# Pairwise tower: a clear of 192 in place of 64 scratch columns between gathers, a fourth group looked up by one-hot columns, groups transposed singly

## The reference, cut to what matters

```python
e = stack([tbl_f[ids[:, f]] for f in range(32)], axis=1)      # 1024 x 32 x 64
p, q = e[:, ROW], e[:, COL]                                   # 496 pairs, r < c
kp = einsum('bpj,ipj->bpi', p, kernel)                        # a 64x64 matrix per pair
z = sum(kp * q, axis=-1)                                      # 1024 x 496
h = concatenate([z, dense_ctx], axis=1)                       # 1024 x 512
h = maximum(h @ W_top1 + b_top1, 0); h = maximum(h @ W_top2 + b_top2, 0)
y = h @ W_top3
```

## Time and profile before

| | |
|---|---|
| median of 3 executions | 626.92 us (626.18 to 627.76) |
| profiled execution, its own time | 622.16 us |
| span of its trace | 620.2 us |
| PE, DVE, POOL, ACT busy | 502.4, 305.6, 273.9, 67.4 us |
| mean granted TensorE clock | 0.884 |
| gathers | 244, 950 to 1089 ns each |

### The profile page before, as it was taken

How to read it: one execution, slowest core, us unless ns; L and a number is a source line. 1 busy time by engine, 2 the same in 40 slices (tenths; PEclk the granted TensorE clock), 3 DMA queues, 4 the chain that set the end, 5 groups by cost and what they waited for, 6 DMA issues and landing times.

```text
span 620.2 us, 10322 instructions
## 1 busy us (share of the span) xinstructions
PE 502.4 (81%) x4290; PEld 309.4 (50%) x4290; DVE 305.6 (49%) x324; ACT 67.4 (11%) x130; POOL 273.9 (44%) x492
## 2 busy tenths in 40 slices
PE   1764444589999786678898768699889999999998
PEld 0432200356666454446565435466566666766443
DVE  3611200166776364337455436467377788787000
ACT  0001000011111021011001001011001211100112
POOL 5888887555557676352727445555700000000000
PEclk9975655599999998798978879899989999999999
DMA  5521212033331111010101011010100030000000
GB/s 154 179 71 23 58 23 61 18 90 90 104 109 43 31 24 26 13 25 9 22 16 23 15 23 28 17 22 17 22 12 1 14 110 10 2 10 2 0 0 0
DMA packets 15318, 23.56 MB, mean 38 GB/s; under 512 B 5506, under 2 KB 7810, under 8 KB 15145
## 3 DMA queue, kind: packets, MB, share of 16 engines
q1 hardware_dynamic: 6884, 14.14, 7.8%
q0 software_dynamic: 7808, 8.01, 6.5%
q10 hardware_dynamic: 580, 0.76, 0.4%
HBM read 20.79 MB, written 0.00 MB: 34 GB/s over the span
## 4 chain that ended last, share of the span: by engine, by line
PE 67%; another core or an unknown queue 13%; issue 10%; DVE 7%; DMA 2%; ACT 0%; SPq 0%; DVEq 0%
PE kp L539 37%; PE z_ps L556 19%; DVE prod L485 6%; PE kp L577 4%; PE tr_ps L523 3%; PE kp L583 2%; PE tr_ps L515 2%; DMA k_sb<-in_tbl 2%; DVE prod L495 1%; PE kp L590 0%; ACT pair L397 0%; ACT prod L441 0%; DVEq L484 0%; SPq L334 0%
## 5 line engine op out<-in xcount | busy, mean ns | idle before, releaser
L485 DVE TENSOR_TENSOR prod<-kp,pair 128x1024 f32<-128x1024 f32 x224 | 261.4, 1218 | 239.0 <-PE kp L539 137.7
L539 PE MATMUL kp<-pair,k_sb 64*128 64x256 f32 x1984 | 286.7, 420 | 63.8 <-issue 32.4
L377 POOL DMA_INDIRECT raw<-in_tbl,ids_sb x244 | 232.8, 954 | 174.8 <-PE tr_ps L523 99.9
L539 PEld LDWEIGHTS kp<-pair,k_sb 64*128 64x128 f32 x1984 | 202.8, 203 | 138.8 <-issue 69.5
L556 PE MATMUL z_ps<-prod,ones_sel 128*32 128x256 f32 x1984 | 141.5, 389 | 24.2 <-issue 22.5
L556 PEld LDWEIGHTS z_ps<-prod,ones_sel 128*32 128x32 f32 x1984 | 65.0, 111 | 94.5 <-issue 57.3
L397 ACT ACTIVATE pair<-tr_ps 128x512 f32<-128x512 f32 (+1 forms) x40 | 20.5, 512 | 351.5 <-PE tr_ps L523 249.4
L381 POOL MEMSET rest<- 128x64 f32 x244 | 40.9, 168 | 0.4
L495 DVE TENSOR_TENSOR prod<-kp,pair 128x512 f32<-128x512 f32 x48 | 30.2, 683 | 8.9 <-issue 6.6
L523 PE MATMUL tr_ps<-ident,raw 128*128 128x128 f32 x122 | 23.8, 309 | 11.4 <-issue 10.8
L515 PE MATMUL tr_ps<-prod,k_sb 125*64 125x256 f32 x96 | 16.6, 521 | 15.7 <-DMA k_sb<-in_tbl 13.4
(11 more groups left out here) (10 smaller groups left out, 9.0 us busy)
## 6 DMA issues: line engine op xcount, KB each, us to landing
k_sb<-in_kd SPq DMA_DIRECT2D x15, 512.0 KB, 3.7
raw<-in_tbl,ids_sb POOLq DMA_INDIRECT x244
pair<-pair SPq DMA_DIRECT2D x32, 64.0 KB
k_sb<-in_tbl SPq DMA_DIRECT2D x6, 250.0 KB
k_sb<-in_w SPq DMA_DIRECT2D x1, 1024.0 KB, 5.0
hot_ids_sb<-in_hot_ids SPq DMA_DIRECT2D x3, 250.0 KB
z_sb<-in_dense ACTq DMA_DIRECT2D x1, 512.0 KB
k_sb<-in_w SPq DMA_DIRECT2D x1, 512.0 KB, 5.7
```

What stands on the lines that cost most here:

```text
L377: nc.gpsimd.indirect_dma_start(raw[:, r % RAW_RING, i, n, :], None, tables[f], bass.IndirectOffsetOnAxis(ap=ids_sb[:, 2 * b + i, f:f + 1], ...
L485: nc.vector.tensor_tensor(prod[:, u % PROD_RING, :, :].rearrange("p q (i n) -> p (q i) n", i=UNIT_SLOTS), kp[u % KP_RING][:, :, :].rearran ...
L539: last = nc.tensor.matmul(kp[u % KP_RING][:, q, i * WIDTH:(i + 1) * WIDTH], k_sb[rows, x, :], pair[rows, group_place(st, owner // 2), :], ...
```

## The change

The clear between two gathers covers 192 columns in place of 64. Group 6 of stage 0 joins the groups looked up by one-hot columns: four gathers fewer, 16 more compares on DVE, 16 more matmuls (32 records) on PE, one more load of ids and two of tables on SP. Since `prod` has no room for a fourth set of one-hot columns, that set lies in `k_sb` ahead of the tables. All stages transpose group by group: 64 events in place of 40, with a new table of places.

```diff
-REST = 64
+REST = 192
-STAGES = (1, 2, 2, 2)
+STAGES = (1, 1, 1, 1)
-LOOKUP = (0, 2, 4)
+LOOKUP = (0, 2, 4, 6)
-TRANSPOSE_AT = [0, 0, 0, 1, 2, 4, 7, 10, 13, 17, 23, 25, 31, 36, 41, 47, 52, 57, 64, 69, 75, 85, 93, 98, 109, 114,
-                123, 128, 137, 144, 155, 160, 171, 176, 185, 190, 199, 206, 217, 222]
+TRANSPOSE_AT = [0, 0, 0, 1, 2, 4, 7, 9, 13, 15, 20, 25, 31, 36, 41, 47, 52, 57, 61, 63, 64, 66, 69, 71, 75, 79, 85,
+                87, 93, 98, 103, 109, 114, 119, 123, 125, 126, 128, 131, 134, 137, 141, 147, 149, 155, 160, 165,
+                171, 176, 181, 185, 187, 188, 190, 193, 196, 199, 203, 209, 211, 217, 222, 227, 233]
+        H_SLOTS = 2 * SMALL_C * WIDTH // P
+        hot_last = k_sb[:, SLOTS - T_SLOTS - H_SLOTS:SLOTS - T_SLOTS, :].rearrange(
+            "p a n -> p (a n)").rearrange("p (x n) -> p x n", n=WIDTH)
+
         def hot(i, n, c):
+            if HOT_UNITS * i >= PROD_RING:
+                return hot_last[0:SMALL_P, SMALL_C * n + c, :]
             at = (SMALL_C * n + c) * WIDTH
@@
             load_k(0)
-            load_hot_ids(2)
-            load_tables(2)
+            for i in range(2, len(LOOKUP)):
+                load_hot_ids(i)
+                load_tables(i)
```

## The result

| | before | after |
|---|---|---|
| median of 4 executions | 627.34 us (626.18 to 632.51) | 557.01 us (556.73 to 557.37) |
| span of the trace | 620.2 us | 554.8 us |
| granted clock, mean | 0.884 | 0.938 |
| last gather starts | 448.1 us | 397.3 us |

The ratio is 0.887, with a 95% interval of 0.882 to 0.892. The change is faster by 70 us, where the prediction had 11 and a range down to 590 us. The direction was right and the time was outside the range. Where the executions of one kernel spread by more than 1.5%, as in the first two sessions further down, a ratio compares only those within 1.5% of the fastest of their kernel, while the medians are over all, so the two don't divide out exactly.

What follows compares the result with a forecast made beforehand. Taken as the bound: runs of gathers on POOL hold up PE's instructions and updates. Start +7.0, single events -17.5, stage 0 +0.5, clock -1 make -11 us: 611 against 622.2, given as 616 us; 8-in-10 range 590 to 637.

Steps and rivals of the forecast that it cites:

- What bounds the kernel: Whole kernel: during runs of gathers PE's instructions and semaphore updates get through ever more slowly; a pair of groups costs 5.4 us.
- The price of the clear: POOL, between gathers: 128 more columns cost 0.14 us, so the clear takes 0.30 us and the period is 1.53 us.
- Part 2, the start: Start of the kernel: PE creeps through the first run and has added lookup work left over; +7.0 us, bounds +1 and +15.
- Rival A: Gaps between gathers: the wider gap itself lets PE through, with the creeping rate doubled; 588 us, chance 0.27.
- The form of the first run: POOL's first unbroken run: 76 gathers in place of 80, ending at 121.2 us in place of 116.7.
- Part 3, single events: Stages 1 and 2: group-by-group events split the runs of gathers; 69 us of hold-up against 86.6 before, -17.5 us.
- a single: One group's run of four gathers, apart from other runs: costs 0.8 us, as in stage 0.
- a joined two: Two neighbouring groups whose gathers join to one run of eight: costs 6.0 us.
- long joined runs: Stages 1 and 2, one each: events at 61, 63, 64 and 66, and 62 units on, join to 16 gathers; 16.2 us each.
- B: Rival: runs counted as single join where events are four units apart, costing 21 us; 640 us in all, chance 0.17.
- C: Rival: engines don't hold each other, so splitting runs gains nothing and the longer start and lookup stay; 635 us, chance 0.05.
- The clock: Whole kernel: the granted clock falls less often, 1 us off; above 0.90 from unit 52 to 171.

Runs made afterwards that it cites:

- first two sessions: Follow-up runs on one chip each: parts of the change alone or in pairs, and a clear of 128 columns; the kernel before took 616.9 and 631.1 us.
- single events alone: The kernel before with group-by-group transposing in all stages and the new table of places, clear of 64 columns and three lookups kept: 575.3 us, ratio 0.944.
- third and fifth session: Follow-up runs, mostly of wider or alternating clears and clears in place of gathers, with the kernel before at 449.3 and 447.9 us.

## Why the prediction was wrong, step by step

**What bounds the kernel: right.** DVE and POOL wait because PE's instructions and updates get through slowly beside gathers. Clears in place of gathers gave 451 us against 630. The wording that they "get through more and more slowly, and that what has gathered gets through when the run ends" fits the kernels with a gap of 0.44 us only.

**The price of the clear: nearly right.** 274 ns in place of 0.30 us, a period of 1.50 in place of 1.53:

```profile
L390 POOL MEMSET rest<- 128x192 f32 x240 | 65.9, 274 | 0.3
```

Against 168 ns for 64 columns that is 0.83 ns a column. The prediction's slope of 1.1 came from a clear of one column. The Trainium skill (GPSIMD Engine Reference, section on elementwise cycle accounting) has 1.03 cycles an element; an estimate from that and its clock of 1.2 GHz is 0.86 ns a column, and the trace agrees with it.

**Part 2, the start: this step failed.** "PE meanwhile creeps" at 11% took the rate of 1.67 records a gather over from a gap of 0.44 us to one of 0.58 us. It forecast +7.0 us; unit 9 came 64.3 us earlier, and with the stage behind it, which lost 45.2 us of that again, the gain to unit 57 is 19.1 us. The step bounded the start by +1 and +15 us, both on the same side, though the only thing known of the creeping rate was its value at one gap. A quantity that had been read at one setting, and that the change moves, was given no bound on the side of a gain. Rival A named exactly this mechanism and then doubled the creeping rate; it rose 5.6 times. The argument held against A (four records that start inside a gather, not in a gap) was about single starts, and says nothing of a rate.

**The form of the first run: wrong by the same step.** 76 gathers and an end at 121 us hold only if PE stands still. With the old clear the changed kernel has just that, a first run of 76 gathers that ends at 110.9 us. With the wide clear it is 108 gathers to 166.9 us, and stage 0 from unit 9 on costs 45.2 us more than before, where the prediction had +0.5.

**Part 3, single events: right in sign, too small by a factor of about 2.8, and the larger share of the miss.** To unit 57 the forecast was off by 7.5 + 19.1 = 27 us and here by 31; either alone puts the time below the range. Forecast -17.5 us, measured -48.6 for units 57 to 171, of which single events alone gave -46.5 (259.0 less 212.5). The terms that were mis-sized are the prices of a single (0.8 us) and of a joined two (6.0). Between units 80 and 123 the changed kernel takes 64.8 us for 43 units, 1.3 us more than the free pace, with singles and a two in it:

```profile
234.80:299.60 64.80, 64.16 (x702) 43.16 (x703) 49.48 (x47) 8.50 (x20) 41.71 (x69) 1.00 0.12 23
299.60:344.00 44.40, 37.05 (x310) 20.63 (x309) 20.49 (x21) 6.36 (x14) 35.52 (x58) 0.92 0.14 28
```

The prediction's prices make about 10 us of it. Over both stages, singles and the twos at 85/87 and 147/149 were priced at 24.8 us and took some 2: units 57 to 171 are 42.1 us over the free pace in the changed kernel, and 40.3 of them lie at the two long joined runs, units 60 to 77 and 123 to 140 (46.1 and 44.4 us for 17 units each), which were priced at 44.4 us with the twos beside them. The 0.8 us came from 7.0 us of stage 0 shared out over nine groups; whatever those 7.0 us were, singles beside the same kind of work cost nothing here. The second line is units 123 to 140, the long joined run, which came out as 24 gathers and not 16: 44.4 us for 17 units, 19.3 more than free, where the prediction's formula gives (24 - 4.1) x 1.53 x 0.89 = 27.1 us for 24. One sum of this part was also wrong, without effect: counted in microseconds, the prices given make 72.2 us and so -14.4, not -15.5.

**Rivals.** A (588 us) came nearest and was still too slow. B, runs that join and cost, happened in stages 1 and 2 only at units 123 to 140 and 61 to 77. C, that the engines don't hold each other, is refuted where the hold-up is on: with as busy a POOL but no indirect DMAs the kernel is 179 us faster. But in the third and fifth session it describes the chip as it was. The rule of the Trainium skill that C was built on (Trainium Architecture — The Big Picture, section on what this means for kernel authors) excepts engines with a semaphore between them. DVE does wait for PE's semaphores here, so no run contradicts the rule; it just can't be used to argue that such a wait ends when the work does, as the 5.2 us above show.

**The clock** rose with the work: 0.83 in the window where it had been 0.55. That the low clock had not been what held PE up can be estimated from the earlier trace rows: at the lower of the two levels 32 records took 6.65 us, so 90 would need some 19 of the 76 us.

## What to carry to other kernels

Where a change alters the very quantity that a hold-up depends on (here the gap between gathers), the rate read at the old setting is no bound; leave the range open on both sides, and price the rival that moves it by more than a factor of two. Here runs of four indirect gathers, a few microseconds apart, cost TensorE next to nothing even with a narrow gap (1.4 us in 43 units); a run of 24 with the wide clear cost it two fifths of its pace (17 units in 44.4 us against 25.1), and one of 76 or 80 with the narrow clear nearly all. Before a kernel is tuned round such a hold-up, time it in several sessions: a spacer of 192 or 256 columns that is worth 5 to 17% with it is a loss of 3 to 6% without.

## What the runs showed of the hardware that was not expected

- The same program takes 617 to 631 us in four sessions and 448 to 449 us in two, each time within 3% in itself, one chip number having shown both. What switches it wasn't found. The kernel with a clear of 256 columns has a trace of either kind, and the difference of the spans, 519.9 - 473.1 = 46.8 us, is as large as PE's idle time ahead of products (of the rest, two cancel out: with the hold-up on the products take 17.7 us more and PE waits 14.9 us less ahead of transpositions). First with it on, then off:

```profile
L539 PE MATMUL kp<-pair,k_sb 64*128 64x256 f32 x1984 | 263.1, 403 | 46.7 <-issue 32.7
...
L539 PE MATMUL kp<-pair,k_sb 64*128 64x256 f32 x1984 | 245.4, 393 | 0.0
```

- The gathers themselves are no slower in it. In the same two traces one takes POOL 0.95 us, and their 7,808 packets take 7.9% of 519.9 us and 8.7% of 473.1 us, 41 us both times.
- The rate at which PE's work gets through rises from 1.7 to 13.5 records a gather as the gap goes from 0.44 to 0.60 us; with nothing in the way it is some 17.
- The hold-up reaches ACT too: in the changed kernel it waited 129.5 us for remote, and started a copy 5.0 us after the transposition that it waited for.
